# Row sums' projection added elementwise on VectorE; phi and g change places around the Gram matrix

## The reference

```python
g_x     = conv1x1(g_w, g_b, x_2).T          # [N, CI], CI = 256, N = 1024
theta_x = conv1x1(theta_w, theta_b, x).T    # [N, CI]
phi_x   = conv1x1(phi_w, phi_b, x_2)        # [CI, N]
W  = theta_x @ phi_x / N
y  = (W @ g_x).T
wy = conv1x1(w_w, w_b, y)
out = batchnorm(wy) + x
```

## Time and profile before

| | us |
|---|---|
| median of 3 runs (1041.92 to 1042.0) | 1041.94 |
| span of the profiled execution, first to last instruction | 1041.2 |
| PE busy (5119 matmuls) | 1032.8 |
| DVE busy | 647.8 |
| ACT busy | 490.6 |
| POOL busy | 274.9 |

### The profile page before, as it was taken

One profiled execution on the slowest core, in us unless ns is written; L12 is line 12 of the kernel. 1 busy time (PEld: TensorE's weight loads), 2 busy tenths in 40 slices (PEclk: granted clock), 3 DMA queues, 4 the chain that ended last, 5 costly groups with the idle time before them and its releaser, 6 DMA issues.

```text
span 1041.2 us, 13910 instructions
## 1 busy us (share of the span) xinstructions
PE 1032.8 (99%) x5119; PEld 854.6 (82%) x5119; DVE 647.8 (62%) x923; ACT 490.6 (47%) x843; POOL 274.9 (26%) x235
## 2 busy tenths in 40 slices
PE   8999999999999999999999999999999999999998
PEld 6778888888888887888878888888887888878887
DVE  6994467844588355873558736586365863658625
ACT  7652564436553264533744337453275532655321
POOL 1312351122601236012350124401244012430220
DMA  7536152451424524245242442434433344323512
GB/s 253 162 75 204 63 196 49 106 190 62 162 56 108 181 67 157 61 111 173 81 142 68 112 166 91 132 76 111 158 109 114 82 121 143 123 101 81 130 33 82
DMA packets 80915, 122.06 MB, mean 117 GB/s; under 512 B 13136, under 2 KB 46672, under 8 KB 80848
## 3 DMA queue, kind: packets, MB, share of 16 engines
q1 hardware_dynamic: 71632, 104.39, 32.9%
q10 hardware_dynamic: 9216, 16.78, 5.1%
HBM read 70.79 MB, written 16.78 MB: 84 GB/s over the span
## 4 chain that ended last, share of the span: by engine, by line
PE 95%; DVE 2%; SPq 1%; DMA 1%; ACT 1%; issue 0%; DVEq 0%; ACTq 0%
PE pG L651 34%; PE pG L546 15%; PE pG L662 8%; PE pG L554 5%; PE pG L587 5%; PE pT L684 4%; PE pG L684 4%; PE pG L561 4%; PE pT L493 3%; PE pS L599 2%; PE pS L482 2%; PE pM L630 2%; PE pM L639 2%; PE pT L599 2%; SPq L396 1%; PE pG L567 1%
## 5 line engine op out<-in xcount | busy, mean ns | idle before, releaser
L651 PE MATMUL pG<-pt,vT 128*128 128x512 f32 x1536 | 353.9, 389 | 0.0
L651 PEld LDWEIGHTS pG<-pt,vT 128*128 128x128 f32 x1536 | 286.8, 188 | 58.6
L1063 POOL TENSOR_TENSOR xms<-xr,xms 128x512 fp32r<-128x512 f32 x64 | 89.7, 1401 | 324.6 <-ACT xms L840 324.6
L546 PE MATMUL pG<-wv,x2s 128*128 128x512 f32 x720 | 168.6, 391 | 0.0
L546 PEld LDWEIGHTS pG<-wv,x2s 128*128 128x128 f32 x720 | 134.0, 188 | 30.3 <-issue 2.6
L996 DVE SCALAR_TENSOR_TENSOR xr<-pG,cl,xr 128x512 f32<-128x512 f32 x64 | 47.9, 749 | 170.2 <-PE pG L651 170.2
L840 ACT ACTIVATE xms<-xr 128x512 fp32r<-128x512 f32 x64 | 40.3, 629 | 178.5 <-DVE xr L996 178.5
L967 DVE TENSOR_TENSOR pt<-mv,pt 128x512 fp32r<-128x512 f32 x128 | 90.2, 756 | 39.5 <-ACT pt L811 39.3
L1059 POOL TENSOR_TENSOR ys<-yf,ys 128x256 fp32r<-128x256 f32 x32 | 28.9, 906 | 295.5 <-ACT ys L802 295.5
L811 ACT ACTIVATE pt<-mv 128x512 fp32r<-128x512 f32 x128 | 71.9, 620 | 37.5 <-PE pM L639 27.9
L662 PE MATMUL pG<-xms,wth 128*128 128x512 f32 x384 | 88.3, 389 | 0.0
(11 more groups left out here) (138 smaller groups left out, 1433.7 us busy)
## 6 DMA issues: line engine op xcount, KB each, us to landing
mv<-tp SPq DMA_DIRECT2D x512, 64.0 KB, 2.0
x2T_f<-in_ctx2T_dram SPq DMA_DIRECT2D x32, 512.0 KB, 4.8
xr<-in_x_dram ACTq DMA_DIRECT2D x64, 256.0 KB, 4.6
st<-in_ctx_dram SPq DMA_DIRECT2D x31, 512.0 KB, 5.5
st<-in_x_dram SPq DMA_DIRECT2D x29, 512.0 KB, 4.0
out_dram<-oh SPq DMA_DIRECT2D x32, 256.0 KB, 2.2
out_dram<-xr SPq DMA_DIRECT2D x31, 256.0 KB, 7.7
x_raw<-in_x_dram SPq DMA_DIRECT2D x3, 512.0 KB, 8.0
```

The lines of the kernel that those rows point to most:

```text
L546: last = mm(bank, x2s[:, l, c, 128 * m:128 * m + 128], wv[:, r, c, :], start=(c == 0 and n == 0), stop=(c == 3 and n == 2))
L651: last = mm(bank, vT[:, l, m, 128 * c:128 * c + 128], pt(h)[:, r, m, :], start=(m == 0 and n == 0), stop=(m == 7 and n == 2))
L1063: done(tt(xms(h)[:, c, LO, :], xr[c][:, :], xms(h)[:, c, HI, :].bitcast(F), ALU.subtract), "xlo")
```

## The change

The order of the two projections is turned: `Y` now multiplies the Gram matrix by phi_w^T, and `M` by g_w^T with the weights taken from `wpg` and `ys` as the moving operand. The term with the row sums is now psi = phi_w s + N phi_b, wanted as a row that is the same on all partitions. It is made in two steps. First an elementwise sum over the four blocks and both parts of `wpg`, each times its column of `scol`, into `acc` [128, 256]; then two matmuls with a [128, 128] matrix of ones, which add over the partitions. In batches 1 to 7 the sum is eight dependent operations on DVE, whose low part follows as `accl`. In batch 0 it is made on POOL by sixteen operations, two for each term. `gs`, `gt` and `s` go.

```diff
 LATER pe:
-"k:0 k:1 q:0 q:1 v:0 v:1 gs v:2 S:0 S:1 L:0 L:1 L:2 gt S:2 S:3 ...
+"k:0 k:1 q:0 q:1 v:0 v:1 psi v:2 S:0 S:1 L:0 L:1 L:2 S:2 S:3 ...
 LATER act:
-"x1:1 x1:2 xs:3 x1:3 x2T:0 k x2T:1 x2T:2 x2T:3 x2T:4 x2T:5 s q v:0 ... S:0 L:0 L:1 gs S:1 L:2 L:3 gt S:2 ...
+"x1:1 x1:2 xs:3 x1:3 x2T:0 k acc x2T:1 x2T:2 x2T:3 x2T:4 x2T:5 q v:0 ... S:0 L:0 L:1 S:1 L:2 L:3 S:2 ...
-"... Y:2 Y:3 S:6 ...
+"... Y:2 Y:3 psi S:6 ...
 LATER dve:
-"k q v:0 q2 ...
+"acc k accl q v:0 q2 ...
 LATER pool:
-"... x1:3,1 s x2T:0 ...
+"... x1:3,1 x2T:0 ...
 FIRST pe:
-"... G:3 gs S:4 gt GT:0 v:6 GT:1 v:7 S:5 Y:0 ...
+"... G:3 S:4 GT:0 v:6 GT:1 v:7 S:5 psi Y:0 ...
 FIRST act:
-"... x2T:7 s v:5 ... G:1 gs gt G:2 T:1 G:3 GT:0 S:4 GT:1 w:7 v:6 ... Y:3 S:7 ...
+"... x2T:7 v:5 ... G:1 G:2 T:1 G:3 GT:0 S:4 GT:1 acc w:7 v:6 ... Y:3 psi S:7 ...
 FIRST pool:
-"... x2T:7 s Y:0 ...
+"... x2T:7 acc Y:0 ...

 PE:
+            def do_psi(b):
+                wait(eng, "acclo", b)
+                if b:
+                    wait(eng, "Blo", b - 1, 1)
+                else:
+                    eng.wait_ge(s_ones, 1)
+                    wait_free(eng, b, 3)
+                    wait(eng, "GTlo", b, 1)
+                for part in (HI, LO):
+                    last = mm(psi_bank, ones_r[:, :], accs(b)[:, part, :], start=(part == HI), stop=(part == LO))
+                done(last, "psi")
 do_GT:
-                if r == 0:
-                    wait(eng, "s_colc", b)
 do_M:
+                if k:
+                    wait(eng, "psirow", b)
-                        last = mm(pM[:, k, 0:256], ys[:, l, c, 128 * k:128 * k + 128], wpg[:, r, c, 0:256],
+                        last = mm(pM[:, k, 0:256], wpg[:, l, c, 256 + 128 * k:384 + 128 * k], ys[:, r, c, :],
 ACT:
+            def do_acc(b):
+                wait(eng, "acc", b, 7)
+                done(act(accs(b)[:, HI, :], acc(b)[:, :], ACT.Copy), "acchi")
+            def do_psi(b):
+                wait(eng, "psi", b)
+                wait(eng, "g", b, use_v(b, 7))
+                done(act(psi_row[:, :], psi_bank, ACT.Copy), "psirow")
 DVE:
+            def do_acc(b):
+                wait(eng, "x2sum", b, 3)
+                eng.wait_ge(s_br8, 1)
+                for n in range(8):
+                    c, part = divmod(n, 2)
+                    if n:
+                        wait(eng, "acc", b, n - 1)
+                    done(stt(out=acc(b)[:, :], in0=wpg[:, part, c, 0:256].bitcast(F), scalar=scol[:, c:c + 1],
+                             in1=acc(b)[:, :] if n else br[:, 256:512], op0=ALU.mult, op1=ALU.add), "acc")
+            def do_accl(b):
+                wait(eng, "acchi", b)
+                done(tt(accs(b)[:, LO, :], acc(b)[:, :], accs(b)[:, HI, :].bitcast(F), ALU.subtract), "acclo")
 do_mt:
-                for k in range(2):
-                    done(stt(out=gsum[:, k:k + 1], in0=gsc[:, k, 0:1], scalar=nbg[:, k:k + 1], in1=gsc[:, k, 1:2],
-                             op0=ALU.add, op1=ALU.add), "gsum")
 POOL (batch 0 alone):
+            def do_acc(b):
+                wait(eng, "x2sum", b, 3)
+                eng.wait_ge(s_wlo, W_PG + 1)
+                eng.wait_ge(s_bd, 16)
+                eng.tensor_scalar(br[:, 256:512], br[:, 0:256], N / 128.0, None, ALU.mult).then_inc(s_br8, 1)
+                eng.wait_ge(s_br8, 1)
+                for n in range(8):
+                    c, part = divmod(n, 2)
+                    if n:
+                        wait(eng, "acc", b, n - 1)
+                    eng.tensor_scalar(accp[:, :], wpg[:, part, c, 0:256].bitcast(F), scol[:, c:c + 1], None,
+                                      ALU.mult).then_inc(s_accp, 1)
+                    eng.wait_ge(s_accp, n + 1)
+                    done(tt(acc(b)[:, :], accp[:, :], acc(b)[:, :] if n else br[:, 256:512], ALU.add), "acc")
+                wait(eng, "acchi", b)
+                done(tt(accs(b)[:, LO, :], acc(b)[:, :], accs(b)[:, HI, :].bitcast(F), ALU.subtract), "acclo")
```

More of the change, by code:

```diff
@@ L23 @@
 PER = dict(
-    k=2, q=2, S=8, GT=2, M=2, B=2, g=40, s_row=1, s_col=1,
-    t1k=1, t1q=1, khi=1, qhi=1, vhi=8, exp=8, Thi=8, Ghi=4, Lhi=4, GThi=2, Yhi=4, shi=1, s_rowc=1, s_colc=1, mthi=1, Bhi=2,
+    k=2, q=2, S=8, GT=2, M=2, B=2, g=40, psi=1,
+    t1k=1, t1q=1, khi=1, qhi=1, vhi=8, exp=8, Thi=8, Ghi=4, Lhi=4, GThi=2, Yhi=4, acchi=1, psirow=1, mthi=1, Bhi=2,
     xhi=8, xc=4, thhi=4, x2hi=4, x1hi=4, x2Thi=8,
-    kf=4, qf=2, klo=1, qlo=1, gf=36, mx=8, rec=8, norm=8, tr=8, Tlo=8, Glo=4, GTlo=2, slo=1, gsum=2, mtf=2, mtlo=1, Blo=2,
+    kf=4, qf=2, klo=1, qlo=1, gf=36, mx=8, rec=8, norm=8, tr=8, Tlo=8, Glo=4, GTlo=2, mtf=2, mtlo=1, Blo=2,
     x2sum=4, x2lo=4, oa=4,
-    x2Tlo=8, Ylo=4, xlo=8, x1lo=8,
+    x2Tlo=8, acc=8, acclo=1, Ylo=4, xlo=8, x1lo=8,
 )
@@ L85 @@
     pool=(
-        "x2T:0 x2T:1 x2T:2 x2T:3 x2T:4 x2T:5 x2T:6 x2T:7 s Y:0 Y:1 Y:2 Y:3 PV:0,0 PV:0,1 PV:0,2 PV:0,3 PV:1,0 "
+        "x2T:0 x2T:1 x2T:2 x2T:3 x2T:4 x2T:5 x2T:6 x2T:7 acc Y:0 Y:1 Y:2 Y:3 PV:0,0 PV:0,1 PV:0,2 PV:0,3 PV:1,0 "
         "PV:1,1 PV:1,2 PV:1,3"
@@ L334, in x1s, with acc, accs @@
             return x1s_next if b else x1s_first
+        def acc(b):
+            return acc_next if b else acc_first
+        def accs(b):
+            return accs_next if b else accs_first
         def w_split(i, part):
@@ L708, in do_w @@
                 eng.wait_ge(s_wd[i], 16)
+                if i == W_O:
+                    wait(eng, "psi", 0)
                 act(w_split(i, HI), W_RAW[i], ACT.Copy).then_inc(s_whi, 1)
@@ L780, in do_x2T @@
                 done(act(x2Ts[:, HI, m, :], x2T_raw(b, m), ACT.Copy), "x2Thi")
-            def do_s(b):
-                wait(eng, "x2sum", b, 3)
-                done(act(sst[:, :, HI], scol[:, :], ACT.Copy), "shi")
+            def do_acc(b):
[5 more added lines that the diff above has]
+                done(act(psi_row[:, :], psi_bank, ACT.Copy), "psirow")
             def do_L(b, r):
@@ L793, in do_G @@
                 wait_free(eng, b, use_g(b, r))
+                if b and r >= 2:
+                    wait(eng, "psi", b)
                 done(act(gram[:, HI, r, G_FROM[r]:512], gram_f[r][:, G_FROM[r]:512], ACT.Copy), "Ghi")
@@ L812, in do_T @@
                 done(last, "Thi")
-            def do_gs(b):
-                wait(eng, "qlo", b)
-                wait(eng, "s_row", b)
-                done(act(grow, pM[0:2, 1, 256:512], ACT.Copy), "s_rowc")
-            def do_gt(b):
-                wait(eng, "s_col", b)
-                done(act(gsc[:, :, :], pM[:, 0, 384:388].rearrange("p (k i) -> p k i", i=2), ACT.Copy), "s_colc")
             def do_mts(b):
@@ L849, in _ @@
             do = dict(w=do_w, xr=do_xr, x2=do_x2, x2a=do_x2a, xs=do_xs, x1=do_x1, k=do_k, q=do_q, k2=do_k2, q2=do_q2, v=do_v, S=do_S, L=do_L, G=do_G,
-                      GT=do_GT, Y=do_Y, x2T=do_x2T, s=do_s, T=do_T, gs=do_gs, gt=do_gt, mts=do_mts, B=do_B, xc=do_xc, PV=do_PV,
+                      GT=do_GT, Y=do_Y, x2T=do_x2T, acc=do_acc, psi=do_psi, T=do_T, mts=do_mts, B=do_B, xc=do_xc, PV=do_PV,
                       th=do_th)
@@ L970, in do_mt @@
             def do_mt(b):
-                wait(eng, "s_colc", b)
                 wait(eng, "M", b, 1)
-                if b == 0:
-                    eng.wait_ge(s_nbg, 1)
+                wait(eng, "psirow", b)
                 for k in range(2):
-                    done(stt(out=gsum[:, k:k + 1], in0=gsc[:, k, 0:1], scalar=nbg[:, k:k + 1], in1=gsc[:, k, 1:2],
-                             op0=ALU.add, op1=ALU.add), "gsum")
-                for k in range(2):
-                    wait(eng, "gsum", b, k)
-                    done(stt(out=mtf[:, k, :], in0=br[:, 0:256], scalar=gsum[:, k:k + 1], in1=pM[:, k, 0:256],
+                    done(stt(out=mtf[:, k, :], in0=psi_row[:, :], scalar=gb(k), in1=pM[:, k, 0:256],
                              op0=ALU.mult, op1=ALU.add), "mtf")
```

54 lines of the change are left out of this document (20 added, 34 removed), and 18 rows, old and new, of tables (act, dve, pe).

## The result

The kernel after takes 1053.38 us, median of 4 runs (1052.06 to 1053.39), beside 1041.97 for the kernel before (4 runs, 1041.92 to 1042.54). The ratio is 1.0103, with a 95% interval from 1.0091 to 1.0116: slower, by 11.4 us, where 3.7 us less had been predicted. The profiled execution of after has a span of 1050.3 us and a time of 1052.06, so 1.8 us lie outside the span. The runs of the kernel before beside the experiments show the same 1.8 (1042.24 beside a span of 1040.4). The span of 1041.2 shown ahead of the prediction is therefore a somewhat long execution of before, and that of after is its shortest. Between the two spans lie 9.1 us, and these are what the traces have to explain; the other 2.3 of the 11.4 are the distance of the two profiled executions from their medians.

What follows compares the result with a forecast made beforehand. PE was taken to bound batches 1 to 7, their time being the sum of its matmuls. 1041.2 - 6.3 (PE work) + 0.7 (`S:0`) + 1.9 (batch 0) = 1037.5 span, 1038.2 us with 0.74 added; range 1035.6 to 1040.8.

Steps and rivals of the forecast that it cites:

- PE's removed work: PE, batches 1 to 7: `gs` and `gt` go, `psi` comes, 0.90 us less per batch, -6.3 us in all.
- `M` and `Y` with their operands changed over: PE: counts and shapes stay, only operand roles and `wpg` halves change; priced at nothing.
- Rival D: PE's count falls without time, if wide weights make `psi` dear or `M`'s new operands run slower; chance 0.02.
- A step: DVE, batches 1 to 7: each of `acc`'s eight dependent operations takes 0.42 us, eight take 3.4 us.
- The collision: DVE's `acc` against POOL's `x2T:0`: one per batch, at most 1.26 us, so `acc` ends at about 787.3.
- `klo` and `S:0`: Late `acc` delays DVE's `klo`, for which PE's `S:0` waits; 0.1 us a batch, +0.7 in all.
- Batch 0: +1.9 forecast: Batch 0: late POOL and ACT's `acc` delay `Y:0` by 1.5 us, DVE loses 0.4; between +0.35 and +5.
- POOL's sum: POOL, batch 0: 11.7 us from 45.04, plus 3.5 for four collisions, ending at about 60.3.
- That `psi` falls into the wait: PE, batch 0: PE waits before `Y:0` anyway, and `psi` falls into that wait.
- The 0.74 us: Whole kernel: added between span and median, taking the forecast from 1037.5 to 1038.2.
- B: Rival: the start swallows the gain, batch 0 at +5 and 0.3 a batch at `S:0`, 1042.7 us; chance 0.19.
- C: Rival: slower, `acc` later still and `klo` the bound in each batch at `S:0`; 1049 if it ends at 789; chance 0.06.

Runs made afterwards that it cites:

- e1: Kernel before with only a 352-byte gap ahead of the large buffers; 1051.55 us, ratio 1.0093.
- e2: Kernel after with its small buffers allocated ahead of the weight tiles, undoing only the move; 1045.19 us, ratio 1.0032.
- e9: e2 with POOL's `x2T:0` in batches 1 to 7 waiting for the last step of `acc`; 1042.53 us, ratio 1.0002.
- e3: Kernel after, batch 0 reordered: ACT's `acc` behind `T:3`, PE's `psi` behind `Y:2`, ACT's `w:8` behind its `Y:2`; 1050.43 us, ratio 1.0075.
- e10: e9 with batch 0's eight products made on ACT, POOL keeping the additions, and ACT's `acc` ahead of `T:0`; 1035.48 us, ratio 0.9931.

## Why the prediction was wrong

**PE's removed work: right, and a little small.** Predicted were 0.90 us a batch; the window without collision and move is shorter by 0.99 (128.24 less 127.25); at the slower pace it is 0.85 (129.52 in e1 less 128.67 in after). `psi` costs 0.23 to 0.24, and `M` with its operands changed over costs the same 1.43 for 12.

**The step that failed: the pace of the matmuls that stay.** "So in batches 1 to 7 the time is the sum of PE's matmuls": the sum then had one term for PE, the matmuls removed and added, and took the pace of all others as given, at nothing and without a reason. What the prediction did price at nothing in so many words, `M` and `Y` with their operands changed over, held. The diff moved the large buffers by 352 bytes against the weight tiles, and that costs 1.28 us a batch, shown by the move alone (e1) and by its removal (e2): +9.0 us against the -6.3. Rival D had the right form, PE's count falling without time, but looked for it in `psi` and `M`, the two places where matmuls had been edited, and gave it 1 in 50. The prediction goes through engines, waits and DMAs, and never through the allocations.

**`acc`: right mechanism, step too small.** A step was estimated at 0.42 and is 0.51, inside the bounds 0.375 and 0.585: eight steps are 0.7 us longer. The collision came as forecast, once a batch, at 0.95 us (bounds 0.89 and 1.26). The Trainium skill says in "SBUF — State Buffer", section "Who interferes with whom", that a VectorE instruction with two SBUF inputs contends with a GpSimd instruction that reads SBUF, and that the shared ports are an exclusive lock. These runs agree: seven steps take 3.61 us with no POOL operation between, 4.52 with one and 5.64 with two.

**What is late next: right idea, wrong place.** I followed the delay to `klo` and `S:0` at 0.1 a batch. Most of it bites earlier, at `v:2`, which waits for DVE's low part of `v:0`. Between e2 (127.61) and e9 (127.25) lie 0.36 a batch: 0.24 are in front of `v:2`, 0.11 between `v:2` and `S:0`. `S:0` starts in e2 0.06 behind the end of `klo`, so this smaller part may be the one that was forecast; the rows don't decide it. Batch 1 loses 0.83, and the seven together 3.0 us. I had looked only at `q`, `q2`, `v:1` and `k2` behind it, and not asked which PSUM buffer `v:2` writes. In the kernel after PE is late itself, and the delay shows in batch 1 alone, with 0.34. Its other batches are 0.14 longer than 129.52 - 0.99 = 128.53; no wait and no group of rows holds more than a few hundredths of that, and its cause is open.

**Batch 0: +1.9 forecast, 5.7 measured: right path, one term too small and one missing.** The first is POOL's sum. A one-input operation was taken at 0.5, nearer the cast; the runs show 0.92 undisturbed and 1.24 in the median (L1073), at the upper bound and beyond it. A two-input one takes 0.74, less than the 0.906 used. The sum was 18.65 us long instead of 15.3 and ended at 63.21 instead of 60.3. `Y:0` slipped by 4.33 instead of 1.5, the same 2.9 more, along the path that the prediction names (ACT's `acc`, `v:6`, DVE's low part). That `psi` falls into the wait held too. The second term was not there at all: the standing still brought a lower granted clock, 0.97 us on the first matmuls of `Y`; no step of the prediction had asked what a wait of PE does to its clock. The remaining 0.4 us are not traced. e3, which takes `acc` out of the way, has `Y:0` in time, and e10, which has the sum ready 12 us earlier, loses nothing: between e9 and e10, which differ in batch 0 alone, lie 7.05 us in the medians, and 5.96 between the starts of batch 1's `k` (145.74 and 139.78).

**The sum with the measured terms**, against the span of 1041.2: -6.9 (PE's work) + 9.0 (the move) + 0.3 (the delay at `v:2` in batch 1) + 1.0 (seven times the 0.14 whose cause is open) + 5.7 (batch 0) = 1050.3, the span that was measured. The last three are read from the kernel after itself, so they are not independent of that span; the first two are. The 0.74 us that the prediction added between span and median was no property of the kernel: 1.8 us lie outside the span in the executions here, and the profiled one of before was a long one.

Of the rivals, B (batch 0 swallows the gain, at +5) described that part; C (slower, through `klo`) had the right sign for the wrong reason: no row names a wait for `klo`, and lateness on DVE's side cost 0.3 us here, 3.0 without the move.
